# A tower kernel on one core: attention weights loaded and cast earlier in the token stage, sixteen unused matmuls and the first transposes ahead of the column mean

## The reference

```python
x = _layernorm(patches, ln1_g, ln1_b)            # 64 images x 36 patches x 768
x = einsum('bnp,pd->bnd', x, W_lin) + b_lin      # 192 wide
x = _layernorm(x, ln2_g, ln2_b)
h = concatenate([cls, x], axis=1) + pos          # 37 tokens per image
n = _layernorm(h)
q, k, v = n @ Wq, n @ Wk, n @ Wv                 # 8 heads
h = h + attention(q, k, v, relative positions) @ Wo + bo
h = h + top-2 of 8 experts(_layernorm(h))
```

## Time and profile before

| | |
|---|---|
| median of 3 runs | 615.82 us (614.15 to 616.25) |
| the profiled execution | 611.56 us |
| its span, first to last instruction | 609.7 us |
| PE, DVE, ACT, POOL busy | 89%, 72%, 42%, 36% |
| mean granted PE clock | 0.942 |

### The profile page before, as it was taken

The page is one execution under the profiler, slowest core; times in us unless marked ns, Lnnn a source line. Parts: engine busy times, 40 slices in busy tenths (PEclk is TensorE's granted clock), DMA queues, the critical chain, the costliest instruction groups (busy, mean ns, idle before and its releaser), DMA issues.

```text
span 609.7 us, 12386 instructions
## 1 busy us (share of the span) xinstructions
PE 541.8 (89%) x4264; PEld 501.8 (82%) x4264; DVE 440.9 (72%) x1018; ACT 258.9 (42%) x415; POOL 219.5 (36%) x209
## 2 busy tenths in 40 slices
PE   3999588999999999999999786867999999999983
PEld 2999587998999989989999662445899999999982
DVE  8889955677677677776776857553777777877763
ACT  1222443254243342542443115304685595585560
POOL 0266410201202112012021015028587787777464
PEclk9999796999999999999999677669999999999998
DMA  8798435020211201202112027206276466367151
GB/s 207 175 223 260 123 77 140 15 52 0 51 34 17 51 17 34 51 0 51 34 17 51 2 84 209 83 14 159 54 170 147 106 146 150 91 132 153 19 168 32
DMA packets 62009, 54.97 MB, mean 90 GB/s; under 512 B 29204, under 2 KB 52564, under 8 KB 61182
## 3 DMA queue, kind: packets, MB, share of 16 engines
q1 hardware_dynamic: 52830, 46.04, 29.6%
q0 software_dynamic: 9152, 8.59, 8.4%
HBM read 39.32 MB, written 18.27 MB: 94 GB/s over the span
## 4 chain that ended last, share of the span: by engine, by line
PE 47%; DVE 14%; ACT 13%; issue 10%; SPq 5%; DMA 4%; POOL 3%; DVEq 2%; POOLq 1%; ACTq 0%
PE PS L1043 7%; PE PS L733 6%; PE PS L756 6%; PE PS L712 5%; ACT wide L1088 4%; PE PS L1041 4%; ACT hTh L1231 3%; PE PS L740 2%; PE PS L747 2%; PE PS L749 2%; PE PS L748 2%; DVE hTl L1710 2%; PE PS L1018 2%; ACT b2w L1237 2%; PE PS L720 2%
## 5 line engine op out<-in xcount | busy, mean ns | idle before, releaser
L1761 POOL TENSOR_TENSOR rs<-ve,nhalf 111x1 f32<-111x1 f32 (+2 forms) x40 | 26.1, 653 | 270.0 <-DVE ve L1353 188.1
L1895 POOL DMA_INDIRECT running_sums<-ye,gid x42 | 73.1, 1739 | 35.1 <-DVE ye L1734 25.9
L1043 PE MATMUL PS<-w2hl,hTh 128*128 128x384 f32 (+1 forms) x288 | 82.7, 357 | 0.0
L1041 PE MATMUL PS<-w2hl,hTl 128*128 128x192 f32 (+1 forms) x288 | 73.5, 255 | 4.0 <-DVE hTl L1710 4.0
L1869 POOL DMA_INDIRECT xe<-routed_rows,gid x48 | 53.4, 1112 | 43.7 <-DVE gid L1675 29.5
L1018 PE MATMUL PS<-xeT,w1h 128*128 128x370 f32 x288 | 64.3, 331 | 2.1 <-issue 1.4
L1710 DVE TENSOR_TENSOR hTl<-hf,hTh 128x740 fp32r<-128x740 f32 x48 | 44.6, 929 | 24.7 <-ACT hTh L1231 23.2
L1041 PEld LDWEIGHTS PS<-w2hl,hTl 128*128 128x128 f32 (+1 forms) x288 | 53.7, 186 | 6.3 <-issue 5.6
L712 PE MATMUL PS<-xT,wh 128*128 128x222 f32 x264 | 46.9, 287 | 7.4 <-DVE xT L1367 7.4
L1043 PEld LDWEIGHTS PS<-w2hl,hTh 128*128 128x128 f32 (+1 forms) x288 | 53.0, 184 | 0.5
L1018 PEld LDWEIGHTS PS<-xeT,w1h 128*128 128x128 f32 x288 | 50.4, 188 | 2.8 <-issue 1.8
(11 more groups left out here) (243 smaller groups left out, 1289.8 us busy)
## 6 DMA issues: line engine op xcount, KB each, us to landing
wide<-x SPq DMA_DIRECT2D x24, 288.0 KB, 9.1
w1r<-L_ffn_W SPq DMA_DIRECT2D x16, 384.0 KB, 5.0
rel_scores<-wide SPq DMA_DIRECT2D x66, 73.0 KB
w2r<-L_ffn_W SPq DMA_DIRECT2D x8, 576.0 KB, 4.5
w1r<-L_ffn_W SPq DMA_DIRECT2D x16, 192.0 KB, 4.7
wide<-rel_scores SPq DMA_DIRECT2D x22, 111.0 KB, 2.3
out<-running_sums SPq DMA_DIRECT2D x1, 1776.0 KB, 7.4
h_tokens<-narrow SPq DMA_DIRECT2D x24, 72.0 KB, 2.8
```

The costliest lines, as they stand in the source:

```text
L1041: pe.matmul(PS[0:n, bank, 0:D], hTl[:, c, at], w2hl[:, c, 0, :], start=(c == 0), stop=False, skip_group_check=True)
L1043: last = pe.matmul(PS[0:n, bank, 0:2 * D], hTh[:, c, at], both(w2hl[:, c, :, :]), start=False, stop=(c == HC - 1), skip_group_check=True)
L1895: p_.indirect_dma_start(sums, at, ye[0:r, e % 2, n, :], None, bounds_check=B * T + NT * 128 - 1, oob_is_err=True, compute_op=ALU.add).then ...
```

## The change

SP issues the loads of Wq, Wk and Wv right behind the store of chunk 0, and the stores of chunks 1 and 2 behind them; the wait in front of the weights (the pixels that they overwrite have been used) stays. ACT casts the four pieces of `wh` behind its copies of units 14, 15, 16 and 17. DVE makes the remainders of pieces 0 and 1 one place earlier each, that of piece 0 ahead of the wait for the first group, and that of piece 2 ahead of the statistics of the last chunk. PE starts with sixteen matmuls of `ones` by `ones` into a PSUM bank that nobody reads, which wait for the memsets alone; it transposes unit 0 ahead of the column mean and unit 1 ahead of the wait for `W_cen`.

```diff
-            for q in range(2):
-                sp.wait_ge(s_ht, q + 1)
-                store_rows(q)
+            sp.wait_ge(s_ht, 1)
+            store_rows(0)
             sp.wait_ge(s_tT, 7)
             sp.wait_ge(s_v1, 3)
             load_qkv(Wq, 0)
             load_qkv(Wk, H * K)
-            sp.wait_ge(s_ht, 3)
-            store_rows(2)
             load_qkv(Wv, 2 * H * K)
+            for q in (1, 2):
+                sp.wait_ge(s_ht, q + 1)
+                store_rows(q)
             sp.wait_ge(s_ho[0], 16 * (4 * CHUNKS // 2 + 2))
             load_rows(0, 2)
...
+            pe.wait_ge(s_set, 2)
+            for _ in range(16):
+                pe.matmul(PS[:, 5, 0:128], ones[:, :], ones[:, :], start=True, stop=True)
             pe.wait_ge(s_early, 16 * N_EARLY)
-            pe.wait_ge(s_set, 2)
-
-            pe.wait_ge(s_gw, 1)
-            pe.matmul(PS[:, 6, 0:D], meanw[:, :], wsum[:, :], start=True, stop=True).then_inc(s_mean, 1)
...
             tok_transpose(0)
-            pe.wait_ge(s_wc, 1)
+            pe.wait_ge(s_gw, 1)
+            pe.matmul(PS[:, 6, 0:D], meanw[:, :], wsum[:, :], start=True, stop=True).then_inc(s_mean, 1)
             for u in range(len(units)):
                 if u + 1 < len(units):
                     tok_transpose(u + 1)
+                if u == 0:
+                    pe.wait_ge(s_wc, 1)
                 tok_product(u)
...
-                if u in (UNITS - 2, UNITS - 1):
-                    n = u - (UNITS - 2)
-                    qkv_high(n)
+                if u >= UNITS - 4:
+                    qkv_high(u - (UNITS - 4))
...
             rows_transposed(0)
-            qkv_high(2)
-            qkv_high(3)
             act.wait_ge(s_aw, 16 * N_AW)
...
                 if u == UNITS - 3:
+                    qkv_low(0)
                     dve.wait_ge(s_h, 32)
                     ln1_var(0)
                 if u == UNITS - 2:
                     ln1_rows(0)
-                    qkv_low(0)
-            qkv_low(1)
+                    qkv_low(1)
             rows_low(0)
...
+            qkv_low(2)
             ln2_stats(NH // 2 - 1, 1)
-            qkv_low(2)
             qkv_low(3)
```

## The result

| | before | changed | ratio, 95% interval |
|---|---|---|---|
| median of 12 runs each, us | 614.54 | 618.14 | 1.0069 [1.0054, 1.0084] |
| profiled execution, us | 611.56 | 616.86 | |
| span of it, us | 609.7 | 614.8 | |
| granted clock, mean | 0.942 | 0.937 | |

The forecast was no change, 615.6 us. The time is beyond the 0.3% that a measurement can tell, and on the other side from the small gain that the sum gave. It lies inside the range, near the 619.0 of the first rival.

The account below looks back on a forecast made before the run. The prediction took DVE, from chunk 3's pixels on, to bound the stretch to the first projection. Terms +0.95 - 1.3 = -0.35 us, weighted to -0.2, gave 615.82 - 0.2 = 615.6 us; range 612.6 to 619.0.

Parts of the forecast that it names:

- the small gain that the sum gave: Whole kernel: -0.35 us at the first projection, weighted to -0.2, giving 615.6 us.
- the first rival: Before unit 15: queue drains slower, Wv lands after 58.6, ACT holds units 15 to 17; +3.2 us, 619.0, chance 0.22.
- What bounds the kernel: Up to the first projection: chunk 3's pixels first, then DVE sets the pace; a shift there runs to the end.
- Wv at 56.4: Weights' loads: 3.18 MB at 308 GB/s take 10.3 us from 46, so Wv lands at 56.4 instead of 61.04.
- "3.18 MB have moved": Transfer queue from 46 us: 0.14 MB of pixels, 0.29 of chunk 0 and 2.75 of weights move before Wv lands.
- The product at 2.22: PE at unit 15: product priced at 2.22 us after cast 1.47 and copy 0.80, ending at 60.94.
- The other two rivals: Clock: one half-rate drop vanishes, 613.0 us, chance 0.12; full wait: ACT's whole 4.0 us wait gained, 611.8 us, chance 0.06.
- The landing of the first rows: Load behind the stores, which land by 58.3: rows at 61.6 to 62.9 against 61.70, costing 0 to 0.2, taken as 0.
- The remainders: DVE's list before the first projection: +0.95 for piece 0 earlier, -1.3 for one removed later, sum -0.35 us.
- The opening at 0: PE's start: mean behind six transposes costs 0 to 1.2 us, taken as 0 since sixteen matmuls should raise the clock.
- DVE free at 60.93 and unit 15 ready at 60.94: At unit 15: the two meet; a later Wv adds one for one, an earlier one gives nothing.
- The bounds for Wv: Wv's landing by queue rate: 55.6 at 332 GB/s, 59.1 at 242, 60.9 at 214.

Follow-up runs that it names:

- warm_unit15: The changed kernel with eighteen more unused matmuls just before unit 15's product: ratio 1.0052.
- casts_back: The changed kernel with the four casts put back behind the copies of units 16 and 17 and the first transposed rows: ratio 1.0005.
- own_sems: The changed kernel with Wq, Wk and Wv each counted on its own semaphore, a cast waiting only for its matrix: ratio 1.0006.
- dma_only: The kernel before with the new order of loads and stores alone: ratio 1.0024.
- after_old_opening: The changed kernel with TensorE's opening as before, no unused matmuls and the mean ahead of the first transposes: ratio 1.0076.
- open_matmuls: The kernel before with the sixteen unused matmuls at the opening alone, the mean staying ahead of the first transposes: ratio 1.0022.
- own_sems_old_order: The changed kernel with each matrix on its own semaphore, but loads, stores and opening as before: ratio 0.9977.
- both: The changed kernel with own semaphores, loads, stores and opening as before, and DVE's remainder of piece 1 behind the transposed rows' split: ratio 0.9968 against before.

## Why the prediction was wrong

**What bounds the kernel** was read rightly: DVE from chunk 3 on, and the shift ahead of the first projection reaches the end (5.05 us there, 5.1 in the span of the profiled executions, about 4 in the timed runs).

**Wv at 56.4: the step that failed.** The prediction divided the rates of two stretches by their DMA share, got 332 and 292 GB/s, and took 308. Their middle weighted by length is 303 ((3 x 332 + 8 x 292) / 11). In the changed kernel the queue was full in the same two stretches, at shares of 1.03 and 1.05, and they moved 311 and 267, together 279. Of the 50 GB/s that the division added to the 242 at a share of 0.83, 25 were there. At 279 the 3.18 MB take 11.4 us instead of 10.3, so 57.4: 1.0 us of the 3.57.

**"3.18 MB have moved" was taken for "Wv has landed".** The other 2.6 us. The twelve loads of weights count up their semaphore in 192 pieces, and the cast waits for the last. By the semaphore updates in the trace 173 pieces had landed at 57.4 us and 191 at 59.4; the last came at 59.94. The queue went on meanwhile: the first piece of the two stores behind the weights landed at 57.39, 2.6 us before Wv's last, and 110 of their 128 pieces were there before it. The windows agree: 46 to 57 us moved 0.93 + 2.14 = 3.07 MB and 57 to 60 another 0.70, together 3.77, which is the 3.18 MB and the 0.58 MB of the stores. So Wv's last piece landed when most of what stood behind it had moved as well. Why these last pieces were late isn't shown: the trace doesn't name a piece's DMA engine, and no run takes the stores from behind the weights with all else as it is. The Trainium skill, "DMA: Bandwidth & Descriptors", section "Queues, rings and completion order", says both halves: ring order holds on each DMA engine, and completion is not first in, first out for the issuing engine. The prediction used the first half, concluded that a store can't pass the weights, and left out the second, which this trace shows; the 12.3 us of the earlier trace rows show a full queue, not an order.

**The product at 2.22.** The prediction itself listed PE idle before unit 15 as a sign of the change, 2.5 us of it, and priced the product behind it from a row that followed 2.49 us of idle time. With 5.37 us of idle time the product took 4.15: 1.93 us more, which warm_unit15 gave back. The first rival's price left it out as well.

**The first rival** happened, by its mechanism: Wv later than 58.6, and units queued in ACT's list behind the cast. Its 4.15 us at 214 GB/s lies near the measured loss by chance, since its terms were others. The sum with the right terms: 3.57 (59.97 - 56.4) + 1.93 - 0.35 = 5.15 at the projection, measured 5.05.

**The other two rivals** did not happen. The clock's drop at the projection stayed and came 5 us later with it (granted clock 0.51 from 76.3 to 79.6, shown below). ACT's wait for Wv was not worth its 4.0 us: it was 0.94 in casts_back and at most 1.39 at a time in own_sems, and DVE scaled unit 15 at 23.8 there as before.

**The landing of the first rows** was put at 61.6 to 62.9; it was 64.02 (SP's next issue follows at 64.04), since the stores had landed at 61.39 instead of 58.3. It cost nothing in the changed kernel only because DVE came at 68.19. dma_only and casts_back show its own price, 2.2 us without work in the wait and 0.6 with it.

**The remainders**, -0.35, are borne out: from unit 15's scaling to the projection the changed kernel took 9.91 us (76.35 - 66.44) against 10.46 before (71.30 - 60.84), and own_sems reaches a projection 0.15 us under that of before although its first rows' statistics start 1.3 us later.

**The opening at 0**: the result was right (after_old_opening), the reason was not. The sixteen matmuls were to have the clock up; PE idled 5.37 us behind them and six transposes took 1.51, the slow price; the mean took 0.85, nearer to the 0.98 of before than to the 0.59 of open_matmuls. The mean ended at 14.3, later than the 13.9 of the slow price (the fast one gives 12.7 by these rows, where the prediction has 12.6), and the pixels' wait covered it.

**The weighing** was at fault as much as a number. DVE free at 60.93 and unit 15 ready at 60.94 is a tie at the edge: earlier gives nothing, later is paid one for one. The bounds for Wv, 55.6 to 60.9, lay mostly on the paying side, and the chance of 0.22 didn't reflect that.

## What to carry to other kernels

- A cast moved up an engine's list brings its wait with it, ahead of all that stands behind: give each load its own semaphore before the consumers are spread, so that a consumer waits for its own operand alone. Here that alone turned 1.0069 into 1.0006.
- When two times meet in a sum, look at which side is paid: if early gives nothing and late costs one for one, put the chance of a loss by how much of the uncertain term's range lies on the late side.
- Time a load's last piece, not its bytes: at the 279 GB/s of the full queue, the bytes up to Wv's end are worth 57.4 us; the last piece of Wv landed at 59.94, when most of the stores queued behind it had moved too.

## What the runs showed of the hardware

The windows of the changed kernel that hold PE's first work after two idle stretches, and its first projection (columns as above):

```profile
59.30:66.10 6.80, 3.91 (x12) 3.91 (x13) 1.79 (x5) 5.29 (x5) 2.63 (x3) 0.50 0.25 58
11.50:14.90 3.40, 2.72 (x12) 2.67 (x13) 0.53 (x2) 0.80 (x1) 0.00 (x0) 0.50 0.99 220
76.30:79.60 3.30, 3.25 (x15) 3.28 (x16) 3.10 (x11) 0.74 (x2) 0.38 (x1) 0.51 0.15 38
```

- The granted clock was 0.50 (1.2 GHz) in both stretches that hold PE's first work after 5.37 us of idle time. After 5.39 us of unused matmuls that ended at 6.81, the transposes at 12.18 were at half rate again. The drop from 68.3 to 75.0 that the kernel before had the earlier trace rows is not gone: it came with the projection, whose first three matmuls took 0.93 us, against 0.95 before.
- How long the first projection ran at half rate differed between executions: until 79.6, some 3.3 us, in the changed kernel, but until 80.6 in dma_only and casts_back (granted clock 0.50 from 70.4), which is 5.7 and 6.4 us. So one execution's span doesn't repeat the shift at the projection: dma_only's projection came 2.2 us later than before, and its span from DVE's start on chunk 3 was 3.8 us longer.
- Idle time alone didn't tell the price of the next product of twelve matmuls: 4.15 us after 5.37 of idle time, 4.21 after 3.67 (after_old_opening) and 3.90 after 2.04 (own_sems_old_order), but 2.22 after 2.88 (open_matmuls).
- In the kernel before, the first transposes took 2.98 for 12, 0.25 each, just as in the changed kernel at a granted clock of 0.50 (1.51 for 6). The view gives a granted clock of 1.00 for that stretch of before. So at a program's start the duration of a known instruction told more than the clock's column.
- Wherever DVE made the remainder beside POOL's last operation, it took 1.79 to 1.80 us instead of 0.69, in the kernel before and in the changed one: the collision stayed in the same place, as predicted. The kernel both makes no remainder there: none of those ahead of its projection took more than 0.69, and POOL's operation took 1.40 instead of 1.83.
